# Local attention in blocks of 64 queries instead of 128, eight heads to a bank

## The chip, the cores and the metric

One NeuronCore of a Trainium2 chip runs the whole program. The metric is the time of the program on the device in microseconds (us), the median of several runs; lower is better.

## The reference

The reference is a network of twelve small parts on 4 rows of 512 tokens of width 128, in fp32. The change touches one part, a local attention that is applied twice (two layers `l`) to each row, 8 times in all. Cut to what matters (8 heads of 64, window 64):

```python
q, k, v = split(shift_token(x) @ wqkv)           # 8 heads of width 64
q, k = l2norm(q) * qs, l2norm(k) * ks            # then rotated by position
bq = (q * 8).reshape(b, h, w, 64, 64)            # w = 512 / 64 blocks of queries
bk, bv = look_around(k), look_around(v)          # own block and the one before: 128 keys
sim  = einsum('bhwid,bhwjd->bhwij', bq, bk)
mask = (i < j) | (i > j + 64) | (j == -1)
out  = einsum('bhwij,bhwjd->bhwid', softmax(where(mask, -max, sim)), bv)
```

Its output goes through a projection and is added to x; a small gated MLP (`f0_mlp`) follows each layer.

## The kernel before

The four rows run in two lanes. Lane A computes rows 0 and 2, lane B rows 1 and 3; each has its own four PSUM banks (`ps(0)` to `ps(3)`, 128 partitions x 512 fp32) and its own scratch. A part is written as four Python generators, one for each engine (TensorE, ScalarE, GpSimd, VectorE). `run_lanes` asks them in turn for their next piece: the pieces between two `yield`s of lane A are issued, then one piece of lane B, and so on. The lanes are thus interleaved in a fixed order in each engine's queue, and an engine carries out its queue strictly in that order. Lane B begins with a unit `prepare` and is three pieces behind lane A from then on. All waits are semaphores: `s.at(name, n)` is a wait, `s.up(name)` an increment.

`f0_attn` is the unit that changes. With the numbers of the kernel before, on TensorE it has these pieces:

- the input is transposed to `hT` (L834);
- eight pieces, one for each chunk (four pairs of heads `hb`, for k and then q): two projections with 512 moving columns (L851), and the sums of squares of the chunk before (`norms`, L842: four matmuls that have 128 columns of `sq` as stationary operand and two moving columns). ScalarE squares (L944), VectorE multiplies with the rotation tables (L1014, L1017), GpSimd adds the two products (L995);
- two pieces with two value projections each (L863), which ScalarE copies into `v` (L949). ScalarE also computes the inverse norms `rn` with Ln and Exp (L953, L955), each of which loads an activation table;
- two pieces that spread `rn` over the partitions (L875), after which VectorE scales `kT` (L1030);
- the core loop of 16 steps i = (t, hb) plus two to drain it: 128 queries of tile t, two heads e = 0, 1 of pair hb, 192 keys (128 for t = 0). A step on TensorE is `scores(i)` (L890: queries and keys of the heads lie on partitions 0 to 63 and 64 to 127, the results in banks 0 and 1; L892 adds the band mask by a bf16 matmul), `apply(i-2)` (L913) and `turn(i-1)` (four transposes, L902, two for t = 0). `scores(i)` waits for `exp_ready` of step i-1;
- the output projection (L928).

In the core loop VectorE does for step i, in this order: the reciprocal of the sums (L1040) and the scaling of the probabilities (L1042) of step i-1, once `exp_ready` of i-1 is there, which gives `probs_ready`, the signal that `turn(i-1)` waits for; then, once `scores_in_psum` of i is there, the row maxima (L1048) and the biases (L1049) of step i, which give `max_ready`.

ScalarE does two exponentials with their sums (L969), copies the transposed probabilities (`aT`, L982) and, every fourth step, a finished bank of outputs (`oT`, L975).

Of the kernel before, what the change touches and what calls it, by code (L numbers as in the profile page):

```python
# [15 lines left out]
P = 128  # L16
B = 4
T = 512
# [60 lines left out]
def constants():  # L79
# [35 lines left out]
    j = np.arange(192)  # L115
    ok = (j[None, :] - 64 <= p[:, None]) & (j[None, :] >= p[:, None])
    c["band16"] = halfwords(np.where(ok, 0.0, FAR))
# [684 lines left out]
def f0_attn(net, ln, row, s, sb, enter, l):  # L802
    w, ps, x, y = net.w, ln.bank, net.x[:, row, :, :], ln.y
    HB, N = F0_HB, NT * F0_HB
# [3 lines left out]
    t1 = sb("t1", [P, 2, T])  # L808
    t2 = sb("t2", [P, 2, T])
    qT = sb("qT", [P, HB, T])  # L810
    kT = sb("kT", [P, HB, T])
    ss = sb("ss", [P, 2, HB * NT * 2])
    lnss = sb("lnss", [P, 2, HB * NT * 2])
    rn = sb("rn", [P, 2, HB, NT, 2])
    sq8 = sb("sq8", [P, HB, NT, 2])
    v = sb("v", [P, NT, F0_IN])
    a = sb("a", [P, 3, 2, 256])
    mx = sb("mx", [P, N, 2])
    nmx = sb("nmx", [P, N, 2])
    den = sb("den", [P, N, 2])  # L820
    rden = sb("rden", [P, N, 2])
    aT = sb("aT", [P, 2, 2, 256])
    oT = sb("oT", [P, HB, T])
    keys = lambda t: slice(64 if t == 0 else 0, 192)

    chunk = [(k, hb) for k in "kq" for hb in range(HB)]

    def tensor(pe):
# [9 lines left out]
        def norms(n):  # L838

            pe.wait_ge(*s.at("squares_ready", n + 1))  # L840
            for t in range(NT):
                last = pe.matmul(ps(3)[:, 8 * n + 2 * t:8 * n + 2 * t + 2], sq[:, n % 2, tile(t)], w("halves"), start=True, stop=True)  # L842
            last.then_inc(*s.up("norms_in_psum"))

        pe.wait_ge(*s.at("hT_ready", 2))
        for n, (k, hb) in enumerate(chunk):
            for j, turned in enumerate(("", "s")):
                u = 2 * n + j
                if u >= RING:
                    pe.wait_ge(*s.at("projection_read", u - RING + 1))  # L850
# [6 lines left out]
        for t in range(NT):  # L857
            u = 2 * len(chunk) + t
            if t < RING:
                pe.wait_ge(*s.at("projection_read", u - RING + 1))  # L860
            else:
                pe.wait_ge(*s.at("v_ready", t - RING + 1))
            pe.matmul(ps(u % RING), hT[:, tile(t)], w(f"f0_wv{l}"), start=True, stop=True).then_inc(*s.up("v_in_psum"))  # L863
            if t % 2:
                yield

        pe.wait_ge(*s.at("rn_ready", 1))
        for hb in range(HB):
            if hb == 0:
                pe.wait_ge(*s.at("v_ready", NT))  # L870
            elif hb >= 2:
                pe.wait_ge(*s.at("k_scaled", hb - 1))
            for t in range(NT):
                for e in range(2):
                    last = pe.matmul(ps(hb % 2)[64 * e:64 * e + 64, tile(t)],  # L875
                                     rn[:, 0, hb, t, e:e + 1].to_broadcast([P, F0_HD]), w("ident"), start=True, stop=True)
# [4 lines left out]
        pe.wait_ge(*s.at("rotated", 2 * HB))  # L881

        def scores(i):
            t, hb = divmod(i, HB)
            if i >= 1:
                pe.wait_ge(*s.at("exp_ready", i))
            lo = max(P * t - 64, 0)
            for e in range(2):
                half = slice(64 * e, 64 * e + 64)
# [5 lines left out]
        def turn(i):  # L895
            t = i // HB
            pe.wait_ge(*s.at("probs_ready", i + 1))
            if i >= 1:
                pe.wait_ge(*s.at("aT_ready", i))
            for e in range(2):  # L900
                for c in range(0 if t else 1, 2):
# [1838 lines left out]
```

## Time and profile before

| | before |
|---|---|
| time, median of 3 runs | 3183.99 us (3174.94 to 3184.74) |
| the profiled execution's own time | 3180.16 us |
| its span, first to last instruction | 3178.4 us |
| TensorE busy | 2453.3 us, 77% |
| VectorE busy | 1720.7 us, 54% |
| ScalarE busy | 1016.3 us, 32% |
| mean granted TensorE clock | 0.776 |
| stretch of the eight `f0_attn` units and their MLPs | about 238 to 890 us |

PE is TensorE's matmul side, PEld its weight loads, DVE is VectorE, ACT is ScalarE, POOL is GpSimd. Busy time counts an instruction from its start to its modelled end; matmuls overlap, so that the distance from one group's start to the next one's says more than their length. The granted clock is 1.0 at 2.4 GHz and 0.5 at 1.2 GHz. An fp32 matmul leaves two records, a transpose and a bf16 matmul one.

### The profile page before, as it was taken

How to read it: one execution, taken by the hardware profiler on the slowest of the kernel's cores; microseconds unless marked ns; L12 is line 12 of the kernel's file. 1: busy time of each engine (PE TensorE's matmuls, PEld its weight loads, DVE VectorE, ACT ScalarE, POOL GpSimd, SP SyncE). 2: the span in 40 equal slices, each digit the busy share in tenths (PEclk: the TensorE clock that was granted, in tenths of full speed). 3: DMA queues.
4: the chain of work that ended last, by engine and by line, in shares of the span. 5: the costliest groups of instructions: out<-in, count | busy, mean ns of one | idle time of the engine just before them, and what ended most of it. 6: DMA issues, size and time to landing. Idle time of an engine off the chain costs nothing. (4 is left out here: it accounts for less than half of the span.)

```text
span 3178.4 us, 34176 instructions
## 1 busy us (share of the span) xinstructions
PE 2453.3 (77%) x12610; PEld 1373.0 (43%) x12610; DVE 1720.7 (54%) x4186; ACT 1016.3 (32%) x2008; POOL 582.1 (18%) x484
## 2 busy tenths in 40 slices
PE   4689998999999999998999864755875555566653
PEld 2355665566633333334666653543431211223331
DVE  5544555455532222222353567576348969864657
ACT  1123646364621112112333222222224434222232
POOL 0002020202000000000000043242004415334430
PEclk7879999999975555556999876766667978987775
DMA  3000000000010000000000000000000000000000
GB/s 122 1 10 6 1 1 1 1 1 1 1 69 0 1 1 1 0 1 1 11 1 1 8 1 1 1 1 1 1 1 0 1 0 0 0 1 1 1 1 14
DMA packets 5669, 20.84 MB, mean 7 GB/s; under 512 B 971, under 2 KB 3583, under 8 KB 5119
## 3 DMA queue, kind: packets, MB, share of 16 engines
q1 hardware_dynamic: 5503, 18.66, 1.6%
q8 instruction: 100, 1.64, 0.2%
q14 instruction: 66, 0.54, 0.1%
HBM read 17.61 MB, written 1.05 MB: 6 GB/s over the span
## 5 line engine op out<-in xcount | busy, mean ns | idle before, releaser
L449 POOL TENSOR_SCALAR lane_vare<-lane_mv 128x4 f32<-128x4 f32 x64 | 15.8, 247 | 1781.9 <-DVE lane_mv L443 1781.9
L1325 DVE TENSOR_REDUCE l_attn_lane_mx<-lane_banks 128x2 f32<-128x256 f32 (+3 forms) x128 | 105.5, 825 | 313.8 <-PE lane_banks L1220 312.3
L2065 PE MATMUL lane_banks<-l_attn_lane_hc,base 128*128 128x512 f32 x256 | 137.3, 662 | 115.1 <-DVE l_attn_lane_hc L2220 115.1
L1279 ACT ACTIVATE l_attn_lane_ex<-lane_banks 128x256 f32<-128x256 f32 (+3 forms) x128 | 89.8, 703 | 406.9 <-PE lane_banks L1241 406.9
L2213 DVE TENSOR_TENSOR_SCAN l_attn_lane_h<-l_attn_lane_da,l_attn_lane_u 128x512 f32<-128x512 f32 x128 | 193.5, 1550 | 32.9 <-ACT l_attn_lane_da L2124 27.6
L2147 POOL TENSOR_TENSOR l_attn_lane_u<-l_attn_lane_xp,l_attn_lane_bn 128x512 f32<-128x512 f32 x128 | 153.5, 1219 | 206.8 <-ACT l_attn_lane_bn L2117 206.8
L1239 PE MATMUL lane_banks<-l_attn_lane_q,l_attn_lane_k 9*128 9x384 f32 (+3 forms) x512 | 179.7, 799 | 1.0
L1218 PE MATMUL lane_banks<-l_attn_lane_k,l_attn_lane_q 8*128 8x384 f32 (+3 forms) x512 | 175.8, 783 | 0.0
L1670 PE MATMUL lane_banks<-base,l_attn_lane_sc 128*112 128x128 f32 x256 | 56.4, 360 | 138.0 <-POOL l_attn_lane_sc L1775 99.6
L969 ACT ACTIVATE f_attn_lane_a<-lane_banks,f_attn_lane_nmx,f_attn_lane_sq 128x192 f32<-128x192 f32 (+1 forms) x256 | 125.3, 495 | 70.2 <-DVE f_attn_lane_nmx L1049 69.4
L1431 PEld LDWEIGHTS lane_banks<-weights,l_ffn_lane_hT 128*128 128x128 f32 x1024 | 122.6, 192 | 31.8 <-issue 26.0
L1455 ACT ACTIVATE l_ffn_lane_hT<-lane_banks,weights 128x512 f32<-128x512 f32 x128 | 87.9, 687 | 138.9 <-PE lane_banks L1412 138.6
L1431 PE MATMUL lane_banks<-weights,l_ffn_lane_hT 128*128 128x128 f32 x1024 | 125.5, 276 | 8.3 <-DVE l_ffn_lane_eo L1504 7.1
L851 PE MATMUL lane_banks<-f_attn_lane_hT,weights 128*128 128x512 f32 x256 | 130.8, 637 | 0.4 <-ACT f_attn_lane_hT L938 0.4
L1504 DVE SCALAR_TENSOR_TENSOR l_ffn_lane_eo<-lane_banks,l_ffn_lane_sel,l_ffn_lane_eo 128x128 f32<-128x128 f32 x224 | 63.0, 344 | 120.2 <-PE lane_banks L1431 120.2
L464 PE MATMUL lane_banks<-base,lane_xn 128*128 128x128 f32 x144 | 42.5, 414 | 107.7 <-DVE lane_xn L457 107.6
L2065 PEld LDWEIGHTS lane_banks<-l_attn_lane_hc,base 128*128 128x128 f32 x256 | 46.3, 201 | 181.8 <-DVE l_attn_lane_hc L2220 166.3
L2276 PE MATMUL lane_banks<-l_xattn_lane_km,l_xattn_lane_qT 128*128 128x462 f32 (+1 forms) x192 | 104.4, 650 | 24.9 <-DVE l_xattn_lane_sc L2387 23.0
L1670 PEld LDWEIGHTS lane_banks<-base,l_attn_lane_sc 128*112 128x112 f32 x256 | 35.9, 171 | 155.1 <-POOL l_attn_lane_sc L1775 106.0
L2286 PE MATMUL lane_banks<-base,l_xattn_lane_sc 128*77 128x128 f32 x256 | 54.2, 347 | 61.0 <-POOL l_xattn_lane_sc L2357 61.0
L1048 DVE TENSOR_REDUCE f_attn_lane_mx<-lane_banks 128x2 f32<-128x384 f32 (+1 forms) x128 | 67.0, 524 | 57.1 <-PE lane_banks L892 56.1
L1014 DVE SCALAR_TENSOR_TENSOR f_attn_lane_t<-lane_banks,weights 128x512 f32<-128x512 f32 x64 | 48.0, 750 | 91.2 <-ACT f_attn_lane_sq L944 91.2
(501 smaller groups left out, 5407.8 us busy)
## 6 DMA issues: line engine op xcount, KB each, us to landing
weights<-packed SPq DMA_DIRECT2D x1, 5479.0 KB, 22.3
weights<-packed SPq DMA_DIRECT2D x1, 2320.0 KB, 7.9
weights<-packed SPq DMA_DIRECT2D x1, 2091.0 KB, 12.5
out<-x SPq DMA_DIRECT2D x4, 256.0 KB, 2.2
weights<-packed SPq DMA_DIRECT2D x1, 897.0 KB, 9.9
weights<-packed SPq DMA_DIRECT2D x1, 838.0 KB, 13.8
early<-packed SPq DMA_DIRECT2D x1, 792.0 KB, 8.2
weights<-packed SPq DMA_DIRECT2D x1, 755.0 KB, 4.2
```

What stands on the lines that cost most here:

```text
L851: pe.matmul(ps(u % RING), w(f"f0_w{k}{turned}{l}", tile(hb).start, tile(hb).stop), hT[:, :], start=True, stop=True)\
L969: last = act.activation(a[:, i % 3, e, 64 + k.start:256], ps(e)[:, k], ACT.Exp, bias=nmx[:, i, e:e + 1], scale=sq8[:, hb, t, e:e + 1], acc ...
L1218: pe.matmul(ps(b + e, 0, n), q[r, j, tile(t)], k[r, j, 0:n], start=True, stop=False)
L1239: pe.matmul(ps(e, 0, n), k[r, j, tile(kt)], q[r, j, P * kt:T], start=True, stop=False)
L1279: act.activation(ex[:, kt % 2, h:h + 2, 0:T - P * kt], two(0)[:, :, 0:T - P * kt], ACT.Exp, scale=scale)\
L1325: v.tensor_reduce(mx[:, j, t, h:h + 2], two(h)[:, :, 0:n], AX.X, ALU.max).then_inc(*s.up("row_max"))
L1431: last = pe.matmul(ps(2)[:, tile(t)], hT[:, n % 2, c, tile(t)], w("m1_w2", (2 * (e - 1) + c) * D, (2 * (e - 1) + c + 1) * D), start=(c == ...
L1670: last = pe.transpose(ps(2)[0:C, tile(g)], sc[:, (j // GR) % 2, j % GR, g, :], w("ident"))
L2065: pe.matmul(ps(2 + c), w("ident"), hc[:, c, :], start=(n == 1), stop=(n == NS)).then_inc(*s.up("state_added"))
L2147: g.tensor_tensor(u[:, i % 3, :], dtx[:, c, :], bn[:, n % 2, :], ALU.mult).then_inc(*s.up("u_ready"))
L2213: v.tensor_tensor_scan(h[:, c, :], da[:, i % 3, :], u[:, i % 3, :], 0.0, ALU.mult, ALU.add).then_inc(*s.up("scanned"))
L2276: pe.matmul(score_bank(u), qT[:, tile(t)], km[:, half * H + lo:half * H + hi, :].rearrange("p m k -> p (m k)"), start=True, stop=True).the ...
```

## The change

The core loop goes over 8 blocks c of 64 queries instead of 16 pairs (t, hb). A step holds all eight heads: heads 2 hb on PSUM partitions 0 to 63, heads 2 hb + 1 on 64 to 127, four pairs side by side in one bank, 128 keys each. The bank alternates with c, and `scores(c)` waits for the exponentials of c-2. The mask is one bf16 matmul of 512 columns, issued first. A block's 128 keys start at an odd multiple of 64 for every second block, so the values are projected twice, `va` at tiles of 128 tokens and `vb` shifted by 64; VectorE copies `vb`. The values now have four pieces instead of two. The inverse norms of q are put in the new layout by 16 matmuls with 64 stationary columns in the place of four with 128. VectorE takes the maxima of step c first, and scales the probabilities of step c-1 after them, with one operation of 512 columns. The memset of the padding is gone. `oT` shares its memory with `t1` and `t2`.

```diff
-        for t in range(NT):
+        for t in range(NT):
+            u = PROJ + 2 * t
+            pe.wait_ge(*freed(u))
+            pe.matmul(ps(u % RING), hT[:, tile(t)], w(f"f0_wv{l}"), start=True, stop=True).then_inc(*s.up("va_in_psum"))
+            u += 1
+            pe.wait_ge(*freed(u))
+            if t:
+                last = pe.matmul(ps(u % RING), hT[:, P * t - 64:P * t + 64], w(f"f0_wv{l}"), start=True, stop=True)
+            else:
+                for e in range(2):
+                    last = pe.matmul(ps(u % RING)[half[e], :], hT[:, 0:64], w(f"f0_wv{l}"), start=True, stop=True)
...
         def norms(n):
...
+                for c in range(W):
+                    for e in range(2):
+                        last = pe.matmul(ps(3)[half[e], 8 * n + c:8 * n + c + 1], sq[:, n % 2, block(c)], w("halves", e, e + 1),
+                                         start=True, stop=True)
...
-        def scores(i):
-            t, hb = divmod(i, HB)
-            if i >= 1:
-                pe.wait_ge(*s.at("exp_ready", i))
-            for e in range(2):
-                pe.matmul(ps(e)[:, keys(t)], qT[half, hb, tile(t)], kT[half, hb, lo:P * t + P], start=True, stop=False)
-            for e in range(2):
-                last = pe.matmul(ps(e)[:, keys(t)], net.w16("ident16"), net.w16("band16")[:, keys(t)], start=False, stop=True)
+        def scores(c):
+            if c >= 2:
+                pe.wait_ge(*s.at("exp_ready", c - 1))
+            bank = ps(c % 2).rearrange("p (b k) -> p b k", b=HB)
+            pe.matmul(bank, net.w16("ident16"), bc(band[:, min(c, 1), :], HB), start=True, stop=False)
+            for hb in range(HB):
+                for e in range(2):
+                    keys = slice(0 if c else 64, P)
+                    last = pe.matmul(bank[half[e], hb, keys], qT[half[e], hb, block(c)], kT[half[e], hb, max(64 * c - 64, 0):64 * c + 64],
+                                     start=False, stop=(hb == HB - 1))
...
+        def turn(c):
+            pe.wait_ge(*s.at("probs_ready", c + 1))
+            if c >= 1:
+                pe.wait_ge(*s.at("aT_ready", c))
+            for hb in range(HB):
+                last = pe.transpose(ps(2)[:, tile(hb)], a[:, c % 3, hb, :], w("ident"))
+        def apply(c):
+            for hb in range(HB):
+                for e in range(2):
+                    last = pe.matmul(ps(3)[half[e], P * hb + 64 * (c % 2):P * hb + 64 * (c % 2) + 64], (va if c % 2 else vb)[:, t, f],
+                                     aT[:, c % 2, hb, half[e]], start=True, stop=True)
...
-        for i in range(N + 2):
-            if i < N:
+        for i in range(W + 2):
+            if i < W:
                 scores(i)
             if i >= 2:
                 apply(i - 2)
-            if 1 <= i < N + 1:
+            if 1 <= i < W + 1:
                 turn(i - 1)
             yield
...
+                for hb in range(HB):
+                    last = act.activation(a[:, i % 3, hb, :], ps(i % 2)[:, tile(hb)], ACT.Exp, bias=nmx[:, i, hb:hb + 1],
+                                          scale=sq8[:, hb, i:i + 1], accum_out=den[:, i, hb:hb + 1])
...
+        for i in range(W + 1):
+            if i < W:
+                v_.wait_ge(*s.at("scores_in_psum", i + 1))
+                st.link(v_.tensor_reduce(mx[:, i, :], ps(i % 2).rearrange("p (b k) -> p b k", b=HB), AX.X, ALU.max))
+                v_.scalar_tensor_tensor(out=nmx[:, i, :], in0=mx[:, i, :], scalar=-1.0, in1=sq8[:, :, i],
+                                        op0=ALU.mult, op1=ALU.mult).then_inc(*s.up("max_ready"))
             if i >= 1:
                 j = i - 1
                 v_.wait_ge(*s.at("exp_ready", j + 1))
                 st.link(v_.reciprocal(rden[:, j, :], den[:, j, :]))
+                v_.tensor_tensor(a[:, j % 3, :, :], a[:, j % 3, :, :], bci(rden[:, j, :], P), ALU.mult).then_inc(*s.up("probs_ready"))
```

## Rows read from the trace of the kernel before

**Rows 1.** The page: busy time by engine, and TensorE in 40 slices

```profile
span 3178.4 us, 34176 instructions
PE 2453.3 (77%) x12610; PEld 1373.0 (43%) x12610; DVE 1720.7 (54%) x4186; ACT 1016.3 (32%) x2008; POOL 582.1 (18%) x484
...
PE   4689998999999999998999864755875555566653
...
PEclk7879999999975555556999876766667978987775
```

**Rows 2.** Busy time of each engine in stretches, granted clock (PEclk)

```profile
262.00:301.00 39.00, 39.00 (x224) 25.31 (x222) 19.23 (x30) 12.07 (x20) 15.19 (x12) 1.00 0.00 1
325.00:358.00 33.00, 33.00 (x298) 20.69 (x297) 23.09 (x88) 28.14 (x91) 0.00 (x0) 1.00 0.01 1
...
950.00:1400.00 450.00, 437.28 (x1768) 165.04 (x1768) 111.10 (x214) 85.10 (x127) 6.49 (x10) 0.53 0.00 1
1800.00:1900.00 100.00, 64.87 (x448) 52.84 (x446) 64.60 (x153) 23.92 (x40) 36.74 (x27) 0.71 0.02 7
1900.00:2000.00 100.00, 55.46 (x460) 40.71 (x453) 71.24 (x150) 24.48 (x32) 32.38 (x20) 0.67 0.00 1
...
2500.00:2600.00 100.00, 52.67 (x136) 20.98 (x135) 83.48 (x139) 36.77 (x56) 27.33 (x30) 0.84 0.00 0
```

**Rows 3.** Timeline of TensorE in the core loop: start, length, line, form

```profile
348.24 0.60 PE L890 MATMUL lane_banks<-f_attn_lane_kT,f_attn_lane_qT 64*128 64x192 f32 x4
348.77 0.34 PE L892 MATMUL lane_banks<-weights,base 128*128 128x192 bf16 x2
349.04 0.66 PE L913 MATMUL lane_banks<-f_attn_lane_aT,f_attn_lane_v 128*64 128x128 f32 x8
349.63 0.66 PE L902 MATMUL lane_banks<-base,f_attn_lane_a 128*128 128x128 f32 x4
350.22 0.60 PE L890 MATMUL lane_banks<-f_attn_lane_kT,f_attn_lane_qT 64*128 64x192 f32 x4
```

**Rows 4.** Timeline of VectorE in the same step, idle time before in brackets

```profile
349.14 0.56 DVE L1048 TENSOR_REDUCE f_attn_lane_mx<-lane_banks 128x2 f32<-128x384 f32 x1 [0.56 <-PE lane_banks L892]
349.74 0.16 DVE L1049 SCALAR_TENSOR_TENSOR f_attn_lane_nmx<-f_attn_lane_mx,f_attn_lane_sq 128x2 f32<-128x2 f32 x1
349.81 0.16 DVE L1040 RECIPROCAL f_attn_lane_rden<-f_attn_lane_den 128x2 f32<-128x2 f32 x1
350.01 0.55 DVE L1042 TENSOR_SCALAR f_attn_lane_a<-f_attn_lane_a,f_attn_lane_rden 128x192 f32<-128x192 f32 x2
```

**Rows 5.** Groups by line and form: busy us, mean ns of one, idle before

```profile
L969 ACT ACTIVATE f_attn_lane_a<-lane_banks,f_attn_lane_nmx,f_attn_lane_sq 128x128 f32<-128x128 f32 x64 | 28.7, 455 | 23.3 <-DVE f_attn_lane_nmx L1049 22.5
L2533 DVE TENSOR_REDUCE l_ffn_lane_mx<-l_ffn_lane_p 128x1 f32<-128x512 f32 x16 | 11.0, 686 | 0.5
L2387 DVE TENSOR_TENSOR l_xattn_lane_sc<-lane_banks,l_xattn_lane_mx 128x462 f32<-128x462 f32 x25 | 15.7, 628 | 0.0
L1030 DVE TENSOR_TENSOR f_attn_lane_kT<-f_attn_lane_kT,lane_banks 128x512 f32<-128x512 f32 x32 | 22.0, 688 | 17.3 <-PE lane_banks L875 16.5
L982 ACT ACTIVATE f_attn_lane_aT<-lane_banks 128x512 f32<-128x512 f32 x96 | 57.3, 598 | 3.1 <-PE lane_banks L902 3.1
```

**Rows 6.** Timeline of TensorE while it projects, at either clock

```profile
253.79 3.07 PE L851 MATMUL lane_banks<-f_attn_lane_hT,weights 128*128 128x512 f32 x4
256.66 1.71 PE L842 MATMUL lane_banks<-weights,f_attn_lane_sq 128*128 128x2 f32 x8
...
263.20 0.95 PE L842 MATMUL lane_banks<-weights,f_attn_lane_sq 128*128 128x2 f32 x8
264.01 1.96 PE L851 MATMUL lane_banks<-f_attn_lane_hT,weights 128*128 128x512 f32 x4
265.81 0.95 PE L842 MATMUL lane_banks<-weights,f_attn_lane_sq 128*128 128x2 f32 x8
```

**Rows 7.** Timeline of TensorE from the first core step to the last

```profile
301.37 0.49 PE L890 MATMUL lane_banks<-f_attn_lane_kT,f_attn_lane_qT 64*128 64x128 f32 x4
...
301.92 1.93 PE L863 MATMUL lane_banks<-weights,f_attn_lane_hT 128*128 128x512 f32 x4
306.14 0.49 PE L890 MATMUL lane_banks<-f_attn_lane_kT,f_attn_lane_qT 64*128 64x128 f32 x4 [2.29 <-ACT f_attn_lane_a L969]
...
307.23 1.97 PE L875 MATMUL lane_banks<-base,f_attn_lane_rn 128*64 128x128 f32 x32
...
366.19 3.74 PE L928 MATMUL lane_banks<-weights,f_attn_lane_oT 128*128 128x128 f32 x32
...
375.58 0.66 PE L913 MATMUL lane_banks<-f_attn_lane_aT,f_attn_lane_v 128*64 128x128 f32 x8 [0.69 <-ACT f_attn_lane_aT L982]
```

**Rows 8.** Timeline: column tiles that all lie on the same 64 columns

```profile
1826.98 1.96 PE L1649 MATMUL lane_banks<-weights,lane_xnT 128*64 128x128 f32 x16
```

More of the change, by code:

```diff
@@ L807, in f0_attn, with block, freed @@
     sq = sb("sq", [P, 2, T])
-    t1 = sb("t1", [P, 2, T])
-    t2 = sb("t2", [P, 2, T])
+    products = sb("products", [P, 2, 2, T])
+    t1, t2 = products[:, 0, :, :], products[:, 1, :, :]
+    oT = products[:, :, :, :].rearrange("p i j t -> p (i j) t")
     qT = sb("qT", [P, HB, T])
     kT = sb("kT", [P, HB, T])
[L812 to L824, printed above, removed]
-    chunk = [(k, hb) for k in "kq" for hb in range(HB)]
+    ss = sb("ss", [P, 16 * HB])
+    logs = sb("logs", [P, 16 * HB])
+    rn = sb("rn", [P, 16 * HB])
+    rnk = rn[:, 0:8 * HB].rearrange("p (b t e) -> p b t e", b=HB, t=NT)
+    sq8 = sb("sq8", [P, HB, W])
+    va = sb("va", [P, NT, F0_IN])
+    vb = sb("vb", [P, NT, F0_IN])
+    a = sb("a", [P, 3, HB, P])
+    mx = sb("mx", [P, W, HB])
+    nmx = sb("nmx", [P, W, HB])
+    den = sb("den", [P, W, HB])
+    rden = sb("rden", [P, W, HB])
+    aT = sb("aT", [P, 2, HB, P])
+    half = [slice(0, 64), slice(64, P)]
+    chunk = [(k, hb) for k in "kq" for hb in range(HB)]
+    PROJ = 2 * len(chunk)
+    def block(n):
+        return slice(F0_WIN * n, F0_WIN * (n + 1))
+    def freed(u):
+        b = u - RING
+        if b < PROJ:
+            return s.at("projection_read", b + 1)
+        b -= PROJ
+        if b < 2 * NT:
+            return s.at("vb_ready" if b % 2 else "va_ready", b // 2 + 1)
+        return s.at("k_scaled", b - 2 * NT + 1)
     def tensor(pe):
@@ L840, in norms @@
             pe.wait_ge(*s.at("squares_ready", n + 1))
-            for t in range(NT):
-                last = pe.matmul(ps(3)[:, 8 * n + 2 * t:8 * n + 2 * t + 2], sq[:, n % 2, tile(t)], w("halves"), start=True, stop=True)
+            if n < HB:
+                for t in range(NT):
+                    last = pe.matmul(ps(3)[:, 8 * n + 2 * t:8 * n + 2 * t + 2], sq[:, n % 2, tile(t)], w("halves"), start=True, stop=True)
+            else:
[3 more added lines that the diff above has]
+                                         start=True, stop=True)
             last.then_inc(*s.up("norms_in_psum"))
@@ L895, in turn @@
[L895 to L901, printed above, removed]
-                    last = pe.transpose(ps(2, 256 * e + P * c, 256 * e + P * c + P), a[:, i % 3, e, tile(c)], w("ident"))
+        band = net.w16("band16").rearrange("p (i k) -> p i k", i=2)
+        def scores(c):
[8 more added lines that the diff above has]
+                                     start=False, stop=(hb == HB - 1))
+            last.then_inc(*s.up("scores_in_psum"))
@@ L919, in tensor @@
+            last.then_inc(*s.up("blocks_done"))
+        for i in range(W + 2):
+            if i < W:
                 scores(i)
@@ L989, in gpsimd @@
             norm_pool(ln, s, g)
-        g.memset(a[:, :, :, 0:64], 0.0).then_inc(*s.up("pad_ready"))
         yield
```

113 lines of the change are left out of this document (38 added, 75 removed).

## The prediction

> **What bounds the kernel now.** I read the page first. TensorE is busy for 77% of the span, VectorE for 54%, ScalarE for 32%, and the slices show that TensorE is busy to nine tenths in the slices of the local attention, the fourth to the twelfth, at a granted clock of 0.9 or more in all but the last [rows 1]. Then the stretches. From 262 to 301 us, where both lanes project, and from 325 to 358 us, where both lanes are in the core loop, TensorE has no idle time at all, and its clock is 1.00 [rows 2]. In the core loop VectorE is busy for 23.09 of 33 us and ScalarE for 28.14; both have room. So in this part every TensorE instruction counts in full, and what counts of the others is only what makes TensorE wait.
>
> The timeline shows how a core step is made up. Scores start at 348.24, the mask at 348.77, `apply` at 349.04, `turn` at 349.63, and the other lane's scores at 350.22: 1.98 us for a lane's step of two heads and 128 queries, of which 0.53, 0.27, 0.59 and 0.59 us are the four groups [rows 3]. VectorE begins the maxima at 349.14, some 0.3 us after the last mask matmul has started, because it waited for it (0.56 us idle); the probabilities of the step before are scaled while TensorE scores [rows 4]. TensorE waits for nobody there.
>
> The groups also give the prices. A record of 128 moving fp32 columns costs TensorE about 0.11 us: four transposes take 0.59 us with about 0.15 for the first load and the change of group. Sixteen records with 64 stationary columns that all lie on the same half of the columns take 1.96 us [rows 8]; thirty-two that alternate between the two halves take 1.97 us (L875) [rows 7]. Two column tiles thus run side by side. So do the row tiles of the scores: four records of 192 columns in 0.53 us [rows 3].
>
> **The change part by part, in TensorE's time for one of the 8 units.**
>
> Values: four more projections of two records with 512 columns. Four such records start 1.72 to 1.80 us apart as a group (264.01 to 265.81) [rows 6], so a projection is 0.86 us, and four are +3.44 us. For the first tile the two half-width matmuls go to different halves and should share their time. The copies of `vb` (about 0.69 us each on VectorE, as L1030 [rows 5]) are behind VectorE's idle time in the projecting stretch, 19.23 busy of 39 us [rows 2]; without that cover they would be 2.8 us a unit.
>
> Norms of q: before, a chunk has 8 records that take 0.81 us [rows 6], 0.11 each for loading 128 columns. After, it has 32 records with 64 columns, alternating between the halves. If loads of the two halves overlap like the streams do, that is 16 pairs at 0.06 us, about 0.9 us: +0.1 a chunk, +0.3 us a unit. If they do not, 32 x 0.06 = 1.9 us, +4.2 us a unit. I take the first, as L875 does 16 pairs of the same tile shape in 1.97 us with twice the columns to stream.
>
> Core loop, TensorE's own work in a step of 8 heads and 64 queries. Mask: 512 bf16 columns, 0.21 us, with 0.1 for the change of shape. Scores: 8 matmuls, 16 records of 128 columns, in pairs of opposite quarters of the array: 8 x 0.107 = 0.86, with the first load 0.91. So the last score matmul starts 1.14 us after the step began, and a step's scores take 1.34 us with the change to the next group. `apply`: 16 records of 64 columns in pairs, 0.5 to 0.6 us. `turn`: four transposes as before, 0.59 us. Sum 2.5 us, times 8 = 20 us, against 12 x 1.98 and four shorter steps (fewer keys) at an estimated 1.3, 29 us. By this count alone the change would win.
>
> But TensorE now waits in every step. Its order is scores(c), apply(c-2), turn(c-1), and `turn(c-1)` needs the scaled probabilities, which VectorE now makes after the maxima of c, and these need scores(c). The round trip, from the start of the last score matmul: 0.28 us until the maxima start (as between 348.86 and 349.14); the maxima of 512 columns 0.69 us (0.56 for 384 [rows 4], 0.686 for 512 of another line [rows 5]); 0.04, then 0.08 to the reciprocal and 0.20 to the scaling [rows 4]; the scaling of 512 columns 0.68 us (0.628 for 462 and 0.688 for 512 [rows 5]); 0.07 until `turn` starts. That is 2.04 us. Behind the scores TensorE has only `apply` to do, 0.6 us; behind the waiting `turn` stand the other lane's scores, and VectorE can't help them either, since it waits for those scores next. A step is 1.14 + 2.04 + 0.59 = 3.77 us for a lane, of which TensorE waits about 1.25. ScalarE doesn't bind: four exponentials with their sums at 0.45 us from start to start, a copy of 0.47 and half a copy of outputs make 2.5 us of 3.77 [rows 5].
>
> A unit's loop: the first step 0.9 (64 keys, no turn), seven steps of 3.77 = 26.4, the two draining steps 1.3 and 0.6: 29.2 us. Before: from 301.37 to 376.24 us both lanes' loops take 74.9 us, in which TensorE also has 1.9 of values, 2.3 of waiting at 303.85, 3.8 of spreading, 3.7 of output projection and 0.9 of the MLP's shift [rows 7]; 62.3 us are left, 31.1 a unit. So -1.9 us a unit.
>
> The wait of 2.29 us at 306.14 [rows 7]: lane A's second scores wait for the first exponentials, which stand behind lane B's two table loads. After, the second scores don't wait for the first exponentials, and lane B's table loads fall on lane A's spreading. It goes, once for each of the four pairs of units: -9 us. Nothing late is put in its place: the exponentials have a step of 3.77 us to catch up.
>
> The missing memset on GpSimd lies beside everything: nothing.
>
> Sum at full clock: 8 x 3.44 = +27.5, 8 x 0.3 = +2.4, 8 x -1.9 = -15, -9: +6 us on the profiled execution's 3180.2, 3186.
>
> **The clock.** The trace shows what clock TensorE is granted in what kind of work. Solid work on the full array: 1.00. Busy 97% of the time, but with operands of 8 or 9 rows (950 to 1400 us): 0.53. Busy 55 to 65% of the time, with narrow tiles and waits in each step (1800 to 2000 us): 0.71 and 0.67. Busy 53% of the time with 512-column matmuls on the full array: 0.84 [rows 2]. The new loop works 2.5 of 3.77 us, and for 0.9 of these on half of the array. It is nearest to the rows of 0.67 to 0.71, so I expect the lower level, 1.2 GHz, in more than half of the steps in which both lanes are in the loop. There 128x512 records and norm loads took 3.07 and 1.71 us a group instead of 1.96 and 0.95 [rows 6]. At this level the 1.14 becomes 2.2 and the 0.59 becomes 1.15: a step of 5.4 us, +1.65. With lanes three pieces apart, 12 full steps of the 14 in a pair of units lie beside the other lane's loop or its light pieces; the first two lie beside spreading. Seven of 12 at the lower level cost 11.6 us, with the first and draining steps 12; four pairs: +48 us. All 12 would cost +80.
>
> **The rivals.** *Clock falls in the loop* (0.47): 3180.2 + 6 + 48 = 3234; the median of the runs lies 4 us above the profiled execution, so I say 3235. Its own range is 3205 to 3265.
>
> *The clock holds* (0.28): the waits are as above, but both levels of work still count as enough. For it: TensorE still works two thirds of each step. Against it: the 55 to 65% rows. 3186, with the median's offset up to 3190.
>
> *Faster* (0.15): the round trip does not hold TensorE, or much less, and its own 2.5 us count. For it: two alternating banks and `scores(c)` free of c-1's exponentials. Against it: the order of VectorE's two operations. 56 full steps x 1.25 us less than 3186 gives 3116. It decides as soon as the probabilities of c-1 are scaled before TensorE has finished `apply(c-2)`; half way gives 3150.
>
> *The score tiles do not run side by side* (0.10): before, the two row tiles write to two banks, and no row shows two of them writing to one. Then 8 pairs cost 1.71 instead of 0.86: 60 steps x 0.85 = +51 us, and at the lower clock more: about 3290. The Trainium skill (TensorEngine Tiling (Array Packing), Gotcha 1: PSUM Pressure) speaks for this: different row tiles cannot access the same PSUM bank at once, which is what the new scores do. By that rule the time would be this rival's. The rows with one bank are of column tiles only, so the trace does not decide it. I give the rule little weight because the two score tiles also differ in their columns and so in the partitions they write.
>
> **How the numbers follow.** A measurement can tell about 0.3% from no change, 3174 to 3194. Faster takes the third case and a little of the second (0.17), same the rest of the second (0.22), slower the first and the last (0.61). Unknown norm loads could add 8 x 3.9 = 31 us to any case. The range 3150 to 3275 leaves out the faster half of the third case and the far end of the last two, about 2 in 10.
>
> **What would show it.** In the core loop, `turn` should wait some 1.2 us for VectorE's scaling in each step, and the scores of one lane's step should start 3.7 to 3.8 us after those of the other's at full clock. The group of score matmuls should have 16 records in 0.9 to 1.1 us; 1.8 would be the last rival. The norms of a q chunk should take 0.9 us, not 1.9. The granted clock between both lanes' first and last core steps should be about 0.7; 1.00 there makes the second case. The 2.29 us wait for table loads should be gone. The prediction fails if TensorE's wait before `turn` is short, or if the clock stays up.

## The result and the profile after

The changed kernel takes 3196.68 us (median of 14 runs, 3188.02 to 3212.28); the kernel before, run beside it on the same chip, 3178.19 us (14 runs). The ratio is 1.0062 [1.0044, 1.0079]: slower by some 18.5 us. The profiled execution took 3196.16 us, with a span of 3194.4. From the page of the kernel after, the busy times by engine and TensorE in 40 slices:

```profile
span 3194.4 us, 35769 instructions
PE 2414.0 (76%) x13711; PEld 1356.1 (42%) x13714; DVE 1680.4 (53%) x3834; ACT 979.2 (31%) x1944; POOL 579.0 (18%) x476
...
PE   4689797979789999999999865655875555566653
...
PEclk7779999999975556556899976766667978987775
```

TensorE is busy for 39 us less than before [rows 1], and the whole takes longer. The fifth, seventh, ninth and eleventh slices are now a 7, where before they were 8 or 9: these are the core loops. The clock row is nearly the one of before.

To see whether only this part changed, I read the first start of the first instruction in it, the copy of `hT`, and the last start of the addition to x that closes it. Per-line view of the kernel after, with duration min/median/max in ns, first and last start in us:

```profile
L961 ACT ACTIVATE f_attn_lane_hT<-lane_banks x8: 590/590/591, 241.8 to 745.2; 64x512 f32<-64x512 f32 x8
L1152 DVE TENSOR_TENSOR x<-x,lane_y x4: 692/692/693, 559.1 to 906.5; 128x512 f32<-128x512 f32 x4
```

The same two lines of the kernel before (L936, L1140) read 239.3 and 885.1. The stretch is 906.5 - 241.8 = 664.7 us against 645.8: +18.9 us. The two medians differ by 18.5 us, so this is about the whole difference; I call this part the stretch from here on. Behind it nothing was edited. That part took 2293.3 us before and 2287.9 in the changed kernel, and in the traces of the experiments 2290.0 to 2306.7, whatever the edit. This is why each experiment below is read by its stretch as well as by its ratio. Of the stretch, by stages (windows of the kernel after: length, busy time of PE, PEld, DVE, ACT, POOL with records, clock, DMA share, GB/s):

```profile
262.00:301.00 39.00, 39.00 (x325) 22.05 (x323) 18.89 (x28) 11.92 (x19) 13.90 (x11) 0.98 0.00 1
325.00:358.00 33.00, 22.74 (x332) 17.24 (x333) 15.39 (x37) 22.50 (x86) 0.00 (x0) 1.00 0.01 1
...
240.00:900.00 660.00, 555.51 (x5192) 367.15 (x5193) 308.32 (x672) 292.51 (x812) 98.04 (x91) 0.96 0.01 2
```

Where both lanes project, nothing changed in kind: TensorE has no idle time [rows 2]. Where both are in the core loop, it idles for 10.3 of 33 us, yet its clock is 1.00, not 0.7. Timeline of TensorE there in the kernel after, one step of one lane:

```profile
339.65 0.38 PE L914 MATMUL lane_banks<-weights,base 128*128 128x512 bf16 x1
339.96 1.09 PE L918 MATMUL lane_banks<-f_attn_lane_kT,f_attn_lane_qT 64*64 64x128 f32 x16
340.98 0.69 PE L938 MATMUL lane_banks<-f_attn_lane_aT,f_attn_lane_va 128*64 128x64 f32 x16
342.86 0.66 PE L927 MATMUL lane_banks<-base,f_attn_lane_a 128*128 128x128 f32 x4 [1.19 <-DVE f_attn_lane_a L1062]
343.35 0.38 PE L914 MATMUL lane_banks<-weights,base 128*128 128x512 bf16 x1
```

A step is 343.35 - 339.65 = 3.70 us, with 1.19 us of waiting before `turn`. Sixteen score records take 1.02 us from start to start. VectorE in the same step of the kernel after:

```profile
341.10 0.69 DVE L1055 TENSOR_REDUCE f_attn_lane_mx<-lane_banks 128x4 f32<-128x512 f32 x1 [2.00 <-PE lane_banks L918]
341.82 0.17 DVE L1056 SCALAR_TENSOR_TENSOR f_attn_lane_nmx<-f_attn_lane_mx,f_attn_lane_sq 128x4 f32<-128x4 f32 x1
341.91 0.17 DVE L1061 RECIPROCAL f_attn_lane_rden<-f_attn_lane_den 128x4 f32<-128x4 f32 x1
342.11 0.69 DVE L1062 TENSOR_TENSOR f_attn_lane_a<-f_attn_lane_a,f_attn_lane_rden 128x512 f32<-128x512 f32 x1
```

VectorE waits 2.00 us for the scores, then does 1.7 us of work in a row while TensorE waits for the last of it: each of the two stands idle for the other. The page's group of `turn` gives the total over all steps (count, busy us, mean ns, idle before and its releaser), 71.7 us of waiting:

```profile
L927 PE MATMUL lane_banks<-base,f_attn_lane_a 128*128 128x128 f32 x256 | 42.2, 288 | 71.7 <-DVE f_attn_lane_a L1062 71.7
```

### The profile page after: what moved, and what is told of

It reads as the page before. It is cut to its first block and busy times, and to the rows that moved or that the text cites. A ratio compares the mean times of both kernels' runs of the same rounds, so it can differ in the third digit from the quotient of the medians.

```text
span 3194.4 us, 35769 instructions
## 1 busy us (share of the span) xinstructions
PE 2414.0 (76%) x13711; PEld 1356.1 (42%) x13714; DVE 1680.4 (53%) x3834; ACT 979.2 (31%) x1944; POOL 579.0 (18%) x476
## 5 line engine op out<-in xcount | busy, mean ns | idle before, releaser
L989 ACT ACTIVATE f_attn_lane_a<-lane_banks,f_attn_lane_nmx,f_attn_lane_sq 128x128 f32<-128x128 f32 x256 | 113.6, 455 | 103.7 <-DVE f_attn_lane_nmx L1056 103.7
L927 PE MATMUL lane_banks<-base,f_attn_lane_a 128*128 128x128 f32 x256 | 42.2, 288 | 71.7 <-DVE f_attn_lane_a L1062 71.7
L1055 DVE TENSOR_REDUCE f_attn_lane_mx<-lane_banks 128x4 f32<-128x512 f32 x64 | 44.3, 691 | 95.7 <-PE lane_banks L918 95.7
```

The lines of the kernel that those rows point to most:

```text
L989: last = act.activation(a[:, i % 3, hb, :], ps(i % 2)[:, tile(hb)], ACT.Exp, bias=nmx[:, i, hb:hb + 1], scale=sq8[:, hb, i:i + 1], accum_o ...
```

## The experiments

Each ratio is against the kernel before, run beside it on the same chip; each "stretch" is that of one profiled execution. Ratios tell whether the whole moved, the stretch says more finely where. Two kernels were profiled twice: experiment 1 has a stretch of 603.4 and 604.5 us, experiment 7 of 597.9 and 592.1, so a few us between two stretches mean nothing. For some readings I go finer still and add up "the loops": four pieces, one for each pair of units, each from the start of the first core step to the start of the last `apply`. They are 298.4 us together in the kernel before and 277.3 in the changed one.

**1. VectorE's order in the changed kernel.** The scaling of step c-1 is put before the maxima of step c.

```diff
         for i in range(W + 1):
-            if i < W:
-                v_.wait_ge(*s.at("scores_in_psum", i + 1))
-                st.link(v_.tensor_reduce(mx[:, i, :], ps(i % 2).rearrange("p (b k) -> p b k", b=HB), AX.X, ALU.max))
...
             if i >= 1:
                 j = i - 1
...
+            if i < W:
+                v_.wait_ge(*s.at("scores_in_psum", i + 1))
+                st.link(v_.tensor_reduce(mx[:, i, :], ps(i % 2).rearrange("p (b k) -> p b k", b=HB), AX.X, ALU.max))
...
             yield
```

> The changed kernel with one thing undone: VectorE scales the probabilities of step c-1 before it takes the maxima of step c. Theory (TensorE's wait before turn is the round trip over VectorE, and it is there because of this order): the 1.19 us wait goes, a lane's step falls from 3.70 to about 2.55 us (TensorE's own work, ScalarE's is as long), 56 full steps x 1.15 = -64 us against the changed kernel, about 3132. Rival (the wait before turn only comes first of several; ScalarE's exponentials or the copies would take its place at once): under 15 us gained, step above 3.4 us. Clock at 1.00 in the loop in either case.

Measured: 3149.52 us, ratio 0.9883 [0.9862, 0.9905], stretch 603.4 us, 61 less than the changed kernel. Window and timeline of TensorE in this kernel:

```profile
325.00:358.00 33.00, 30.56 (x442) 24.03 (x439) 18.50 (x44) 30.23 (x114) 0.00 (x0) 1.00 0.01 2
```

```profile
338.40 0.38 PE L914 MATMUL lane_banks<-weights,base 128*128 128x512 bf16 x1
338.71 1.09 PE L918 MATMUL lane_banks<-f_attn_lane_kT,f_attn_lane_qT 64*64 64x128 f32 x16
339.73 0.69 PE L938 MATMUL lane_banks<-f_attn_lane_aT,f_attn_lane_va 128*64 128x64 f32 x16
340.35 0.66 PE L927 MATMUL lane_banks<-base,f_attn_lane_a 128*128 128x128 f32 x4
340.84 0.38 PE L914 MATMUL lane_banks<-weights,base 128*128 128x512 bf16 x1
```

The wait before `turn` is gone from this step, which is 2.44 us, TensorE's own work. In other places a smaller wait takes its place. From the view of waits in this kernel (total us, times, longest):

```profile
PE lane_banks L938 <- ACT f_attn_lane_aT L1001: 20.0, 20, 2.1
```

`apply` now waits 20.0 us in all for ScalarE's copies of the transposed probabilities; in the changed kernel it was 5.3. 56 full steps by 1.26 us would be 71 us; 61 are seen, and these 14.7 us are enough for what is missing. The rival expected this wait to eat up nearly all of the gain, and that did not happen. A second set of runs gave 3149.92 us, ratio 0.9877 [0.9856, 0.9898], stretch 604.5 (below).

**2. The other way round: the changed kernel's order in the kernel before.** VectorE takes the maxima of i before it scales i-1; nothing else differs from the kernel before.

```diff
         for i in range(N + 1):
+            if i < N:
+                t, hb = divmod(i, HB)
+                v_.wait_ge(*s.at("scores_in_psum", i + 1))
...
             if i >= 1:
...
-            if i < N:
-                t, hb = divmod(i, HB)
-                v_.wait_ge(*s.at("scores_in_psum", i + 1))
...
             yield
```

> The kernel before, with only the order of VectorE's two operations exchanged as the change does it (maxima of step i first, then the scaling of step i-1). Theory: the same round trip appears, turn waits for VectorE in each of the 16 steps: a step grows from 1.98 to about 3.0 us, about 96 x 1.0 + 32 x 0.8 = +120 us against the kernel before, about 3300. Rival (the order matters only with two alternating banks): no change, 3178. If the clock falls as I had forecast for such a loop, more than +150 us and a granted clock well under 1.00 between 325 and 358 us.

Measured: 3355.16 us, ratio 1.0527 [1.0503, 1.0551], stretch 806.0 us, +160. A step went from 1.98 [rows 3] to 2.97 us. Timeline and windows of this kernel (its L1049 is the scaling):

```profile
375.44 0.66 PE L902 MATMUL lane_banks<-base,f_attn_lane_a 128*128 128x128 f32 x4 [0.91 <-DVE f_attn_lane_a L1049]
...
378.41 0.66 PE L902 MATMUL lane_banks<-base,f_attn_lane_a 128*128 128x128 f32 x4 [0.91 <-DVE f_attn_lane_a L1049]
```

```profile
325.00:358.00 33.00, 27.71 (x141) 15.33 (x140) 11.62 (x45) 15.25 (x48) 0.00 (x0) 0.51 0.00 1
358.00:378.00 20.00, 14.03 (x126) 8.50 (x124) 9.04 (x34) 11.51 (x35) 0.00 (x0) 1.00 0.01 1
```

The order costs the old tiling 5%, with what the clock does then. With half as much work in a step, the same kind of round trip comes 128 times instead of 64. Waits of TensorE in this kernel (total us, times, longest):

```profile
PE lane_banks L902 <- DVE f_attn_lane_a L1049: 97.9, 120, 1.3
```

In the kernel before this wait is 3.0 us in all, so waiting makes 95 of the 160 us. Most of the rest goes with the clock, which did fall here: to 0.51 from 325 to 358 us, behind waits of 0.9 to 1.3 us, and it was back at 1.00 after that. In the other three pairs of units it stood at about 0.50 for 30 to 50 us.

**3. The second values narrow.** 64 of the 512 columns of `vb` are projected, so 7/8 of it is left out.

```diff
-                last = pe.matmul(ps(u % RING), hT[:, P * t - 64:P * t + 64], w(f"f0_wv{l}"), start=True, stop=True)
+                last = pe.matmul(ps(u % RING)[:, 0:64], hT[:, P * t - 64:P * t + 64], w(f"f0_wv{l}", 0, 64), start=True, stop=True)
...
-                    last = pe.matmul(ps(u % RING)[half[e], :], hT[:, 0:64], w(f"f0_wv{l}"), start=True, stop=True)
+                    last = pe.matmul(ps(u % RING)[half[e], 0:64], hT[:, 0:64], w(f"f0_wv{l}", 0, 64), start=True, stop=True)
```

> The changed kernel, with the second projection of the values for 64 of its 512 columns only (it leaves out seven eighths of vb; all waits and copies stay). Theory (TensorE has no slack in the projecting pieces, so the added records count in full): each of the 32 projections costs 0.11 instead of 0.86 to 0.9 us, -24 to -27 us against the changed kernel, about 3171. Rival (they are behind other waits): within 5 us of the changed kernel.

Measured: 3185.86 us, ratio 0.9999 [0.9983, 1.0015], stretch 645.7, 19.0 less than the changed kernel. That is less than the expected 24 to 27. Most of the miss lies in the price of the narrow form, which still takes 0.17 to 0.26 us. From the norms ahead of the first value projection to the first `turn`, this kernel takes 28.4 us (285.98 to 314.42) and the changed kernel 33.7 (285.71 to 319.41): 5.3 us less for the eight projections of a pair of units, 0.66 each, 21 in all. Only 2 us are left to explain. In one window of this kernel the clock is lower:

```profile
301.00:325.00 24.00, 21.00 (x262) 15.94 (x261) 13.34 (x26) 12.16 (x35) 0.36 (x1) 0.93 0.01 2
```

In the changed kernel the clock of that window is 1.00. The missing matmuls can't be blamed for it: experiments 4, 5 and 6 keep all the value projections, and their clock in this window is 0.93 too.

**4. The old norms of q.** The 16 matmuls with 64 stationary columns are replaced by four with 128, in the order of before; the scales land in the old layout, and so with the wrong queries; the amount of work is that of before.

```diff
-            if n < HB:
+            if True:
                 for t in range(NT):
```

> The changed kernel with the inverse norms of q computed by four matmuls of 128 columns as before (they then lie in the wrong layout, so the outputs are not the reference's; the rest is the same work). Theory (the 32 records of 64 columns cost a q chunk 1.02 us and a change of shape, against 0.81 us, and nothing hides it): about 0.3 us a chunk, 32 chunks, -9 to -10 us against the changed kernel, about 0.3%. Rival, what I had forecast for this edit: -2.4 us, not measurable.

Measured: 3197.97 us beside 3184.5 for the kernel before, ratio 1.0037 [1.0018, 1.0056], stretch 652.6, 12.1 less than the changed kernel. The interval overlaps with the changed kernel's, so only the stretch tells. Timeline of the kernel after, where the norms of a k chunk (L859) and of a q chunk (L863) follow on each other:

```profile
268.17 0.95 PE L859 MATMUL lane_banks<-weights,f_attn_lane_sq 128*128 128x2 f32 x8
268.98 1.96 PE L873 MATMUL lane_banks<-f_attn_lane_hT,weights 128*128 128x512 f32 x4
270.88 1.10 PE L863 MATMUL lane_banks<-weights,f_attn_lane_sq 128*64 128x1 f32 x32
...
301.07 1.13 PE L882 MATMUL lane_banks<-weights,f_attn_lane_hT 128*128 128x512 f32 x2
302.03 1.02 PE L887 MATMUL lane_banks<-weights,f_attn_lane_hT 128*128 128x512 f32 x2
302.98 1.10 PE L863 MATMUL lane_banks<-weights,f_attn_lane_sq 128*64 128x1 f32 x32
```

The old form takes 0.81 us (268.17 to 268.98). The new one takes 1.02 (302.98 to the next group at 304.01), and the projections ahead of it 1.90 (268.98 to 270.88) instead of 1.80: 0.30 a chunk, 1.2 us a unit, 10 us in all. Of the stretch's 12.1 us, 2.8 lie behind the last `apply`, where nothing differs. The loads of the two halves do overlap (32 records in 1.02 us, where the prediction's count without overlap is 1.9), but not for nothing.

**5. A longer wait.** The scaling is done twice, the first time into a spare tile, so that TensorE's wait grows by one VectorE operation of 0.69 us.

```diff
+                st.link(v_.tensor_tensor(spare[:, :, :], a[:, j % 3, :, :], bci(rden[:, j, :], P), ALU.mult))
                 v_.tensor_tensor(a[:, j % 3, :, :], a[:, j % 3, :, :], bci(rden[:, j, :], P), ALU.mult).then_inc(*s.up("probs_ready"))
```

> The changed kernel with VectorE's scaling done twice in each step (once into a spare tile), so that TensorE's wait before turn grows from 1.19 to about 1.95 us. Theory A (the clock holds here too): a step of 4.45 us, 56 to 60 x 0.75 = +42 to +45 us against the changed kernel, clock 1.00 in the loop. Theory B (the changed kernel was near the point at which the clock falls, as I had forecast for it): the clock in the loop falls below 0.8 and the steps at 1.2 GHz take about 6 us, +90 to +130 us.

Measured: 3300.18 us, ratio 1.0352 [1.0329, 1.0375], stretch 753.5, +88.8 over the changed kernel. Window and timeline of this kernel:

```profile
325.00:358.00 33.00, 21.74 (x227) 16.45 (x221) 15.83 (x34) 16.45 (x62) 0.00 (x0) 0.69 0.00 1
```

```profile
340.52 0.66 PE L928 MATMUL lane_banks<-base,f_attn_lane_a 128*128 128x128 f32 x4 [1.92 <-DVE f_attn_lane_a L1064]
341.01 0.58 PE L915 MATMUL lane_banks<-weights,base 128*128 128x512 bf16 x1
341.52 1.97 PE L919 MATMUL lane_banks<-f_attn_lane_kT,f_attn_lane_qT 64*64 64x128 f32 x16
...
346.02 1.11 PE L928 MATMUL lane_banks<-base,f_attn_lane_a 128*128 128x128 f32 x4 [2.53 <-DVE f_attn_lane_a L1064]
346.93 0.63 PE L915 MATMUL lane_banks<-weights,base 128*128 128x512 bf16 x1
```

At full clock a step is now 4.45 us; 56 times +0.75 is 42 of the 88.8 us. The other 47 go with the clock. In the steps in which it is down, the scores take about twice as long (1.97 us as a group) and a step 5.92 us (341.01 to 346.93). This is the picture that the prediction drew of the changed kernel itself, at a wait 0.7 us longer.

**6. The score tiles apart.** The four score matmuls on partitions 0 to 63 are issued first, then the four on 64 to 127, instead of by turns.

```diff
-            for hb in range(HB):
-                for e in range(2):
+            for e in range(2):
+                for hb in range(HB):
```

> The changed kernel with the score matmuls of a step in another order: first the four of the heads on partitions 0 to 63, then the four of the other half. Theory A (the two quarters of the array work side by side only where the queue offers them next to each other): the group takes about 1.7 instead of 1.02 us, a step 4.4 to 4.5 us, the clock falls as with the longer wait, +90 us or more. Theory B (they run side by side in any order, as the four apply matmuls of the kernel before, which came in the order first half, first half, second half, second half): no change, within 5 us of the changed kernel.

Measured: 3270.69 us, ratio 1.0263 [1.0227, 1.0299], stretch 724.1, +59.4. Timeline of this kernel in the loop of the first pair of units, and in that of the second:

```profile
344.36 1.58 PE L918 MATMUL lane_banks<-f_attn_lane_kT,f_attn_lane_qT 64*64 64x128 f32 x16
345.87 0.69 PE L938 MATMUL lane_banks<-f_attn_lane_aT,f_attn_lane_va 128*64 128x64 f32 x16
347.74 0.66 PE L927 MATMUL lane_banks<-base,f_attn_lane_a 128*128 128x128 f32 x4 [1.18 <-DVE f_attn_lane_a L1062]
...
511.63 0.66 PE L927 MATMUL lane_banks<-base,f_attn_lane_a 128*128 128x128 f32 x4 [1.80 <-DVE f_attn_lane_a L1062]
...
512.44 2.65 PE L918 MATMUL lane_banks<-f_attn_lane_kT,f_attn_lane_qT 64*64 64x128 f32 x16
...
524.51 2.88 PE L918 MATMUL lane_banks<-f_attn_lane_kT,f_attn_lane_qT 64*64 64x128 f32 x16
...
529.18 1.11 PE L927 MATMUL lane_banks<-base,f_attn_lane_a 128*128 128x128 f32 x4 [0.75 <-DVE f_attn_lane_a L1062]
```

Windows of this kernel (length, busy times, clock in the third column from the end):

```profile
325.00:358.00 33.00, 24.11 (x303) 19.23 (x302) 13.70 (x32) 19.24 (x73) 0.00 (x0) 1.00 0.00 1
...
530.00:540.00 10.00, 9.25 (x64) 7.16 (x63) 1.92 (x5) 3.66 (x13) 0.00 (x0) 0.50 0.01 2
```

The group takes 1.51 us instead of 1.02 (344.36 to 345.87). By the prediction's 0.107 us a record, sixteen in a row would be 1.71 us and eight pairs side by side 0.86. So the two tiles share their time almost wholly when they are issued by turns, and only in small part, if that price holds for them, when they are issued apart. That is +0.49 a step, 29 us over 60 groups. The other 30 go with the clock. Where both lanes are in the loop, the first pair of units ran at 1.00. The second ran at 0.50 from about 515 to 560 us and the third from about 704 to 741 us, in a cycle of 6.15 us with TensorE busy for up to 9.25 of 10 us. The fourth fell for a few us only. So one and the same loop, with the changed kernel's own wait of 1.18 us at full clock, was seen at both levels. In the second, third and fourth pair the clock fell in the step behind a `turn` that had waited for 1.80 us (at 511.63, 702.43 and 879.85), the longest wait in the loop. The first pair has such a wait too, at 343.56, and its clock stayed up, so this wait alone does not decide it.

**7. The reordered kernel with a copy moved.** Experiment 1, and the copy of the outputs (`oT`) goes from ScalarE to VectorE.

```diff
-                act.wait_ge(*s.at("blocks_done", 2 * (t + 1)))
-                act.activation(oT[:, :, tile(t)], ps(3).rearrange("p (b t) -> p b t", b=HB), ACT.Copy).then_inc(*s.up("oT_ready"))
+                v_.wait_ge(*s.at("blocks_done", 2 * (t + 1)))
+                v_.tensor_copy(oT[:, :, tile(t)], ps(3).rearrange("p (b t) -> p b t", b=HB)).then_inc(*s.up("oT_ready"))
```

> The kernel with the order exchanged (scaling before maxima) and, besides, the copy of the finished outputs moved from ScalarE to VectorE. Theory (with the wait gone the loop is bound by TensorE at 2.44 us a step, and ScalarE, 30.2 of 33 us busy, holds it back now and then): 5 to 12 us less than with the order alone, about 1.4% under the kernel before. Rival (VectorE's copy waits for apply and so delays the next maxima, TensorE waits again): 10 us or more above the order alone.

Measured: 3141.69 us, ratio 0.9846 [0.9805, 0.9887], stretch 597.9. Repeated:

> The order exchanged and the copy of the finished outputs on VectorE once more: ratio to the kernel before 0.983 to 0.987, 5 to 12 us under the order alone; if ScalarE was no bound at all, the same as the order alone within 3 us.

3136.24 us (6 runs), ratio 0.9828 [0.9802, 0.9854], stretch 592.1. This is the fastest version that leaves nothing out. Experiment 1 repeated beside it:

> The kernel with the order exchanged once more, on one chip with the next one, for the interval between the two and against the kernel before: ratio to the kernel before 0.986 to 0.990.

3149.92 us, ratio 0.9877 [0.9856, 0.9898], stretch 604.5. The two intervals do not quite meet, and the medians are 0.4% apart. The traces say it more surely. The loops take 208.7 and 208.6 us in the two sets with the copy moved, 219.3 and 219.8 in the two with the order alone, and `apply` waits 10.0 us in all for ScalarE's copies instead of 20.0. So the copy gains 11 us in the loops. The whole stretch shows 5.5 and 12.4 less, as its other parts differ by some us between traces. Window of the kernel with the copy moved (first set):

```profile
325.00:358.00 33.00, 32.52 (x484) 25.41 (x481) 24.76 (x56) 28.61 (x113) 0.00 (x0) 1.00 0.01 2
```

Against experiment 1 ScalarE gave up 1.6 us, VectorE took 6.3 on, and TensorE is busy for 32.5 of 33 us instead of 30.6.

**8. Half of the longer wait.** As in experiment 5, but the added operation has 256 columns.

```diff
+                st.link(v_.tensor_tensor(spare[:, 0:2, :], a[:, j % 3, 0:2, :], bci(rden[:, j, 0:2], P), ALU.mult))
```

> The changed kernel with one more VectorE operation of 256 columns in each step before the scaling, so that TensorE's wait before turn grows from 1.19 to about 1.6 us and a step from 3.70 to about 4.1. Theory A (the clock falls step by step with the share of the wait, and the changed kernel stands just above the point): the clock is below 1.00 in part of the loop, more than the +0.42 x 58 = +24 us of the wait itself, about +45 to +70 us against the changed kernel. Theory B (it falls only further on): +24 us and a clock of 1.00 in the loop.

Measured: 3231.46 us, ratio 1.0134 [1.0097, 1.017], stretch 693.4, +28.7. Timeline and window of this kernel:

```profile
350.42 0.66 PE L928 MATMUL lane_banks<-base,f_attn_lane_a 128*128 128x128 f32 x4 [1.65 <-DVE f_attn_lane_a L1064]
...
354.58 0.66 PE L928 MATMUL lane_banks<-base,f_attn_lane_a 128*128 128x128 f32 x4 [1.65 <-DVE f_attn_lane_a L1064]
```

```profile
325.00:358.00 33.00, 20.37 (x260) 15.08 (x260) 16.09 (x42) 20.70 (x77) 0.00 (x0) 0.90 0.01 1
```

A step is 4.16 us, +0.46; 56 of them are 26 us. The loops take 312.2 us, 35 more than in the changed kernel, so some 9 us go with the clock, which fell for short pieces. The other parts of the stretch, in which nothing differs, were 6 us shorter in this trace. So this lies between the two theories.

**9. Experiments 1 and 3 together.** With TensorE nearly always at work, the second values should cost in full.

> The kernel with the order exchanged (scaling before maxima), and the second projection of the values for 64 of its 512 columns only (it leaves out seven eighths of vb). With the order alone the projecting pieces are TensorE's in full. Theory: 32 projections x about 0.75 to 0.8 us, -24 to -26 us against the order alone, in the stretch of the local attention and in the whole. Rival (the rows of the earlier run, 19 us less in the stretch, are all that there is because the projections are partly hidden in any case): -18 to -20 us.

Measured: 3131.88 us, ratio 0.9801 [0.9765, 0.9837], stretch 593.2, 10 to 11 less than experiment 1. Windows from 240 to 830 us of this kernel, then of experiment 1:

```profile
240.00:830.00 590.00, 537.78 (x5199) 369.82 (x5200) 310.51 (x679) 287.57 (x814) 99.34 (x93) 0.94 0.01 2
```

```profile
240.00:830.00 590.00, 542.88 (x5176) 361.82 (x5176) 306.49 (x664) 285.82 (x803) 95.94 (x88) 0.97 0.01 2
```

The miss has two parts. From the norms ahead of the first value projection to the first `turn`, this kernel takes 28.1 us (288.28 to 316.35), experiment 1 32.6 (282.96 to 315.60): 4.6 less for a pair of units, 18 in all, not 24 to 26. The narrow form has its price, as in experiment 3, and the first `turn` waits for 1.44 us instead of 0.75: there the projection had kept TensorE at work while it would have waited otherwise. The other 7 to 8 us go with a lower clock, 0.94 against 0.97. But the second set of experiment 1 has 0.96 in this window, and that the narrow matmuls lower the clock is not shown. The whole's ratio moved by 0.8%, about 24 us, but the two intervals are too wide to decide between 10 and 24.

**10. Experiments 1 and 4 together.**

> The kernel with the order exchanged, and q's inverse norms by four matmuls of 128 columns as before (in the wrong layout for q, the outputs are not exactly the reference's). Theory: 32 chunks x 0.3 us = -9 to -10 us against the order alone. Rival, my forecast's term: -2.4 us.

Measured: 3141.79 us, ratio 0.9855 [0.9826, 0.9884], stretch 590.9, 12.5 less than experiment 1 and 13.6 less than its second set. The intervals of the ratios overlap. By the stretch, the new norms cost about the same with the wait and without it.

## Why the prediction was wrong, and where it was right

Slower was right, and 3196.68 us lies in the range, but the forecast of 3235 stood 51 us above the median of before, and 18.5 were measured. That it lies in the range is no merit of the sum: the range was wide because of the clock. Without its clock term the prediction had 3186 to 3190 and called that "same"; what made it slower are two terms that were too small (values and norms, below).

**The step that failed is the clock.** "It is nearest to the rows of 0.67 to 0.71, so I expect the lower level" put +48 us on the loop. The clock of the core loop was 1.00, not the 0.71 and 0.67 that I took over from another part [rows 2], and over 240 to 900 us it is 0.96, where the kernel before has 0.97. The four loops took 68.5, 68.5, 70.1 and 70.1 us; the two longer ones have a short piece at the lower clock, 3 us together (the kernel before has one such piece, of 1.6). So in the loops the term measured under 2 us, not 48. The rival "the clock holds", which I gave 0.28, is what happened. The mistake was to carry a clock over from a part with other tiles and other gaps by its busy share alone. It was not far off: with the wait 0.46 us longer the clock is 0.90, with 0.75 longer 0.69, and with the same wait and the score tiles issued apart it fell to 0.50 in two of four pairs of units for some 40 us each. Why the changed kernel stays on the upper level is open; the runs show only how near the lower one is.

**The round trip was right.** Forecast: a step of 3.77 us with 1.25 of waiting; measured 3.70 and 1.19. Its cause, VectorE's scaling behind the maxima, is shown from both sides: taking it out of the changed kernel gives 61 us back, and putting it into the old one costs 160. So of the change's parts this one decides the sign (experiment 1's ratio; its stretch, 42 us below that of before, says the same): with the old order the new tiling is 1.2% faster than before, not 0.6% slower.

**The loop's sum was right.** In the kernel after, the loops of the first pair of units take from 313.46 to 382.6 us, 69.1 us; without 1.8 of values, 3.8 of spreading, 3.6 of output projection and 0.9 of the MLP's shift 59.0 are left, 29.5 a unit (forecast 29.2; before 31.1). Over 8 units -13, forecast -15. The wait of 2.29 us for the table loads is gone in all four pairs, as forecast; -9 stands. Together these are -22, and the loops of all four pairs went from 298.4 to 277.3 us, -21. TensorE's own step, 2.44 us in experiment 1, was forecast at 2.5.

**The values were sized a little low.** Forecast 0.86 us a projection; `va` to `vb` is 0.96, and `vb` to the next group 0.95 or, ahead of a projection of k or q, 0.86. At 0.86 to 0.95 for each of the 32 added ones this is +28 to +30 against +27.5. The two half-width matmuls of the first tile do share their time: their four records take 0.91 to 1.01 us.

**The norms of q were mis-sized.** Forecast +0.3 us a unit, +2.4 in all. The rows give 0.30 a chunk, 1.2 a unit, 10 in all; the stretch gave 12.1 and 12.5 us. I had counted 16 pairs at 0.06 and left out the changes of shape on both sides of the group. The comparison with L875 was wrong, too: its records stream 128 columns each where those of the norms stream one, so it said little about the loads.

Together: +28 to +30 for the values, +10 to +12 for the norms, -13 and -9 make +16 to +20, where the stretch shows +18.9 and I had summed +6.

**The rival with the score tiles fell.** The group takes 1.02 us (forecast 0.9 to 1.1), not 1.8. By the Trainium skill (TensorEngine Tiling (Array Packing), Gotcha 1: PSUM Pressure) different row tiles cannot access the same PSUM bank at once. Here they write different partitions of one bank and run side by side, so the trace does not agree with the rule taken that widely; experiment 6 shows that it is their order in the queue which matters.

## What to carry to other kernels

When two engines hand work back and forth in fixed queues, write down for each step what stands ahead of the operation that the other engine waits for. An operation whose inputs were ready long ago belongs before one that waits for the newest result; that swap was worth 61 us here, where the tiling itself was worth 42 (stretch 645.8 to 603.4, both in the old order). Then look who waits next: there it was `apply`, for ScalarE, and moving one copy took 11 us off the loops. When work is made larger per step, price the changes of tile shape at either side of each small group, and issue the matmuls of two halves of the array by turns. And don't carry a granted clock over from another part by busy share: lengthen the wait a little and look how far the fall is.

## What was unexpected of the hardware

The clock of a loop can have two answers for the same instructions. In experiment 6 a step of 4.18 us with 1.18 us of waiting ran at 1.00 where both lanes of the first pair loop; in the second pair the clock fell behind a wait of 1.80 us and was at 0.50 for about 45 us. There the wait was only 0.75 us and TensorE was busy for 9.25 of 10 us, and the clock stayed down until, at about 560 us, lane A drained and its last pieces ran with no wait between them. What tipped it is open: the first pair has the wait of 1.80 us as well.

The clock differs between two traces of one and the same kernel. The two of experiment 1 show 0.87 and 0.95 from 240 to 280 us, and 0.97 and 0.90 from 500 to 600 us. So a few hundredths between the traces of two kernels need not be an effect of an edit.

Eight fp32 matmuls on opposite quarters of the array, all into one PSUM bank, take 1.02 us at the full clock issued by turns and 1.51 issued as four and four.
